# One bank and one ScalarE copy for the transposes of a head pair's first two units

## The reference

```
xn  = layernorm(x)
q, k, v = xn Wq + bq, xn Wk + bk, xn Wv + bv         16 heads of 64
att = softmax(causal(q k^T / 8)) / 8                 512 x 512 per head
y   = (att v, heads side by side) proj
ffn = xn W^T + gate-weighted low-rank experts of ranks 1, 2, 4, 8 (top 1 of 4)
out = x + y + ffn
```

## Time and profile before

| what | value |
|---|---|
| median of three executions | 1382.9 us |
| profiled execution, its own time | 1383.64 us |
| span of its trace | 1381.9 us |
| PE busy | 1364.5 us (99% of the span) |
| PE weight loads busy | 1163.6 us (84%) |
| DVE busy | 1110.2 us (80%) |
| ACT busy | 1076.5 us (78%) |
| POOL busy | 973.1 us (70%) |

### The profile page before, as it was taken

How to read it: one execution, slowest core, us unless ns; L and a number is a source line. 1 busy time by engine, 2 the same in 40 slices (tenths; PEclk the granted TensorE clock), 3 DMA queues, 4 the chain that set the end, 5 groups by cost and what they waited for, 6 DMA issues and landing times.

```text
span 1381.9 us, 34974 instructions
## 1 busy us (share of the span) xinstructions
PE 1364.5 (99%) x11053; PEld 1163.6 (84%) x11053; DVE 1110.2 (80%) x4009; ACT 1076.5 (78%) x3161; POOL 973.1 (70%) x1421
## 2 busy tenths in 40 slices
PE   6999999999999999999999999999999999999998
PEld 5788888888888888888888888888888888888887
DVE  4978878788787887878788787887878878788784
ACT  4887877877787787787878878777787877878784
POOL 6777766777677777767777677776676776677664
PEclk7999999999999999999999999999999999999999
DMA  5444444445445444444454544454454444534441
GB/s 143 98 112 114 106 116 109 108 113 117 108 100 125 107 100 120 109 117 97 111 124 100 122 109 108 107 120 112 93 123 114 102 112 111 123 93 116 115 101 47
DMA packets 113011, 151.41 MB, mean 110 GB/s; under 512 B 18303, under 2 KB 47294, under 8 KB 112830
## 3 DMA queue, kind: packets, MB, share of 16 engines
q1 hardware_dynamic: 112830, 149.17, 45.7%
HBM read 10.69 MB, written 4.19 MB: 11 GB/s over the span
## 4 chain that ended last, share of the span: by engine, by line
PE 96%; DVE 0%; POOL 0%; issue 0%; ACT 0%; DVEq 0%; POOLq 0%
PE zp L1187 22%; PE ptp L1163 20%; PE scores L1151 13%; PE jobp L1066 12%; PE scores L1154 12%; PE outp L1199 7%; PE jobp L1071 6%; PE jobp L1081 1%; PE outp L1208 1%; PE jobp L1086 1%; PE jobp L1224 0%; PE jobp L1076 0%; PE outp L1213 0%; PE outp L1284 0%; POOL prob L582 0%; DVE prob L884 0%
## 5 line engine op out<-in xcount | busy, mean ns | idle before, releaser
L582 POOL TENSOR_TENSOR prob<-prob,rden 128x128 f32<-128x128 f32 (+3 forms) x1024 | 711.7, 722 | 345.9 <-DVE rden L873 344.2
L884 DVE CUSTOM_DVE_ANT_0 prob<-scores,mask 128x128 f32<-128x128 f32 (+3 forms) x1024 | 465.3, 487 | 216.4 <-issue 190.4
L667 ACT ACTIVATE prob<-prob,nmax 128x128 f32<-128x128 f32 (+3 forms) x1024 | 564.3, 555 | 35.2 <-DVE nmax L884 35.1
L1163 PE MATMUL ptp<-ident,prob 128*128 128x128 f32 x2560 | 369.9, 274 | 2.0 <-POOL prob L582 1.1
L1151 PE MATMUL scores<-k_twice,q_parts 128*128 128x128 f32 (+3 forms) x1024 | 331.5, 334 | 2.8 <-DMA k_twice<-k_hi 1.7
L1154 PE MATMUL scores<-k_low,q_parts 128*128 128x128 f32 (+3 forms) x1024 | 322.4, 324 | 0.0
L1163 PEld LDWEIGHTS ptp<-ident,prob 128*128 128x128 f32 x2560 | 294.7, 141 | 30.6 <-issue 7.0
L1187 PE MATMUL zp<-pt,v_sb 128*64 128x64 f32 (+3 forms) x4096 | 307.8, 303 | 0.2 <-ACT pt L678 0.2
L678 ACT ACTIVATE pt<-ptp 128x128 f32<-128x128 f32 (+3 forms) x512 | 220.4, 431 | 111.9 <-PE ptp L1163 111.9
L1187 PEld LDWEIGHTS zp<-pt,v_sb 128*64 128x64 f32 x4096 | 221.5, 137 | 51.5 <-issue 19.3
L1151 PEld LDWEIGHTS scores<-k_twice,q_parts 128*128 128x128 f32 x1024 | 193.2, 189 | 69.0 <-issue 43.8
(11 more groups left out here) (163 smaller groups left out, 1697.2 us busy)
## 6 DMA issues: line engine op xcount, KB each, us to landing
k_twice<-k_hi SPq DMA_DIRECT2D x512, 128.0 KB, 2.3
q_parts<-q_hi SPq DMA_DIRECT2D x256, 128.0 KB, 2.3
q_parts<-q_lo SPq DMA_DIRECT2D x256, 128.0 KB, 2.4
xin<-in_L_attn_x_dram SPq DMA_DIRECT2D x16, 256.0 KB, 3.8
xres<-in_L_attn_x_dram SPq DMA_DIRECT2D x16, 256.0 KB, 3.1
out_dram<-osb SPq DMA_DIRECT2D x15, 256.0 KB, 2.6
pt<-in_L_attn_Wq_dram SPq DMA_DIRECT2D x1, 512.0 KB, 4.5
pt<-in_L_attn_Wk_dram SPq DMA_DIRECT2D x1, 512.0 KB, 4.8
```

The lines of the kernel that those rows point to most:

```text
L582: nc.gpsimd.tensor_tensor(part, part, scale, ALU.mult).then_inc(pn_ready, 1)
L667: nc.scalar.activation(part, part, ACT.Exp, bias=nmax[:, s % NROT, h:h + 1], scale=-1.0, accum_out=den[:, s % NROT, h:h + 1]).then_inc(p_r ...
L884: nc.vector.tensor_tensor_reduce(out=prob[:, s % NROT, h, 0:cols], in0=scores[h][:, 0:cols], in1=mask[:, S - cols:S], scale=-INV_SCALE, sc ...
L1163: done = nc.tensor.transpose(ptp[h][:, P * j:P * j + P], prob[:, s % NROT, h, P * j:P * j + P], ident[:])
```

## The change

For the first two units of a pair (`SHARED = 2`) the transposes of both heads go into `ptp[0]`, side by side: 2 x 128 columns for the first unit, 2 x 256 for the second, which fills the bank. ACT waits for both heads and copies both in one instruction, 256 or 512 columns wide; DVE copies nothing for these units. The third and fourth unit stay as they were. PE's transposes of head 1 wait for nothing of their own in the first two units, since head 0's wait covers the bank; in the third and fourth unit they wait for `pt_ready[1]`, which now counts two copies a pair (`wide`). At a pair's first unit ACT waits for the older pair's head 1 `values` in place of head 0's.

```diff
+SHARED = 2
+    def wide(self, p, n):
+        return self.at(UNITS // 2, 2 * p + n)
             def evacuate_pt(c, s):                                  # ScalarE
-                act.wait_ge(t_ready, c.head(s, 0))
                 i, p = s % NBLK, s // NBLK
                 if i == 0:
-                    wait(act, pv_ready, c.values(p - 2, 0))
+                    wait(act, pv_ready, c.values(p - 2, 1))
+                if i < SHARED:
+                    act.wait_ge(t_ready, c.head(s, 1))
+                    src = ptp[0][:, 0:2 * width(s)].rearrange("p (h j q) -> p h j q", h=2, q=P)
+                    nc.scalar.activation(pt[:, p % 2, :, 0:i + 1, P * i:P * i + P], src, ACT.Copy)\
+                        .then_inc(pt_ready[0], 1)
+                    return
+                act.wait_ge(t_ready, c.head(s, 0))
             def evacuate_pt(c, s):                                  # VectorE
+                i, p = s % NBLK, s // NBLK
+                if i < SHARED:
+                    return
                 dve.wait_ge(t_ready, c.head(s, 1))
-                i, p = s % NBLK, s // NBLK
-                if i == 0:
-                    wait(dve, pv_ready, c.values(p - 2, 1))
...
-            evacuate_pt(c, -3)                                      # VectorE, at the very end
             def transpose(c, s):                                    # TensorE
+                i, p = s % NBLK, s // NBLK
                 for h in range(2):
                     pe.wait_ge(pn_ready, c.head(s, h))
-                    wait(pe, pt_ready[h], c.unit(s - 1))
-                    for j in range(s % NBLK + 1):
-                        done = nc.tensor.transpose(ptp[h][:, P * j:P * j + P], prob[:, s % NROT, h, P * j:P * j + P],
+                    if h == 0:
+                        wait(pe, pt_ready[0], c.unit(s - 1))
+                    elif i >= SHARED:
+                        wait(pe, pt_ready[1], c.wide(p, i - SHARED))
+                    dst = ptp[0][:, h * width(s):(h + 1) * width(s)] if i < SHARED else ptp[h][:, 0:width(s)]
+                    for j in range(i + 1):
+                        done = nc.tensor.transpose(dst[:, P * j:P * j + P], prob[:, s % NROT, h, P * j:P * j + P],
                                                    ident[:])
                     done.then_inc(t_ready, 1)
             def values(c, p, h):                                    # TensorE
-                pe.wait_ge(pt_ready[h], c.unit(NBLK * p + NBLK - 1))
+                pe.wait_ge(pt_ready[h], c.unit(NBLK * p + NBLK - 1) if h == 0 else c.wide(p, NBLK - SHARED))
```

## The result

The changed kernel takes 1391.59 us (median of 6 runs, 1390.09 to 1392.52), the kernel before 1382.95 us in the same series. The ratio is 1.0064, with a 95% interval of 1.0054 to 1.0074: slower by 8.6 us, where 9.9 us were forecast. The profiled execution has a span of 1390.8 us, 8.9 us more than before.

A forecast was written before the change was run, and what follows sets the result against it. PE's own work bounds the kernel, with a DVE, ACT, PE chain tight in pairs 1, 3 and 6. Losses of 0.23, 0.16 and 0.23 us, 0.62 us a batch, add 9.9 us to 1382.9: 1392.8 us, range 1384 to 1400 us.

The forecast's parts named there:

- ACT's copy of the second unit: 512 columns for 256, 0.23 us longer; third unit's load late in pairs 1, 3, 6: 0.62 us a batch, 9.9 us.
- the lower bound: At the stalls, PE's loads lose up to 0.05 us less each: about 0.47 us a batch, +7.5 us.
- the pattern comes back in each batch: Third unit tight in pairs 1, 3 and 6 of every batch, read from pair 1 six batches later.
- ACT's copy of the first unit and the wait for both heads: In pairs 0, 2, 4, 7: 0.14 us lateness plus 0.23 us width, 0.37 of 0.51 us slack; no loss counted.
- The load of pair 0 waits too: Sign at the third unit's first load in pair 0: if it waits, the prediction is wrong.
- DVE's relief: DVE loses two copies a pair, some 0.68 us, which ends in its idle time; counted as nothing.
- The rival in which it reaches the fourth unit's maximum: DVE's saved time starts ACT's exponentials earlier in pairs 1, 3, 6: 1377 us, chance 0.09.
- One sign that I had named for it: ACT's idle time before the fourth unit's exponentials in pair 1 shorter than 0.60 us would show DVE's saving arriving.
- PE's waits of head 1: First two units' waits go, 0.24 us in pair 6; PE then waits at the third unit's transposes: nothing counted.
- The dearer copy: Rival: the second unit's two-head copy costs more than its columns, 0.37 us extra: 1400 us, chance 0.13.
- PE taking it up: Rival: at the third unit's loads PE's queue hides the delay, nothing measurable: 1383 to 1385 us, chance 0.16.
- What the prediction took the rule alone to mean: Giving up bank rotation for half the units would make the third unit wait in every pair; rows said three in eight.

The follow-up runs named there:

- e2: Changed kernel with only the second unit sharing the bank (512 columns in one copy), the first unit copied by head as before: 1391.09 us, ratio 1.0063 to the kernel before.
- e3: Changed kernel, ACT waiting for both heads of the second unit but copying only head 0's 256 columns: 1381.33 us, ratio 0.9993 to the kernel before.
- g2: Changed kernel with the second unit's ACT copy cut to 384 columns: 1387.0 us, ratio 1.0027 to the kernel before.
- g1: Changed kernel with both heads of the second unit put into the second bank, ACT's copy as wide: 1380.84 us, ratio 0.9987 to the kernel before.
- e1: Changed kernel with only the first unit sharing the bank (`SHARED = 1`), the second copied by head as before: 1381.08 us, ratio 0.9987 to the kernel before.
- e4: Kernel before without DVE's head 1 copies of a pair's first two units, ACT and banks as before: 1381.3 us, ratio 0.9990.
- f2: Changed kernel with ACT's wide copy of the second unit put before q_hi instead of behind it: 1418.37 us, ratio 1.026 to the kernel before.

## Why the prediction was right

*ACT's copy of the second unit.* This is the step that carries the result, and it held in place and cause, and nearly in number: three pairs in eight, a load 0.11 us behind the wide copy, the others free in the steady batches. e2, e3, g2 and g1 each show a part of it: the unit, the width, its size, the bank. Of the sizes, 0.23 us in pairs 1 and 6 was 0.186 us, or 0.21 us with the next transpose, which is also 0.03 us late. The copy is 0.01 us shorter than the row I took (587 for 597 ns), and the lead of load over matmul gives 0.03 us, where the forecast gave it nothing and the lower bound up to 0.05 us. Pair 3 was forecast at 0.16 us and lost as much as the others: there the wait for head 1 in the second unit went (0.04 us), PE came earlier, and used up the slack that I had counted. With what that wait gave (0.067 us over two transposes) pair 3 is 0.145 us later in all, near the 0.16 us. That the pattern comes back in each batch was wrong for the first one, which the prediction had not read: its pairs 0, 2 and 4 lose 1.05 us together, of which the sum had nothing. The last batch grows by 0.9 us less than a steady one, and that the two ends nearly cancel is luck.

*ACT's copy of the first unit and the wait for both heads, pairs 0, 2, 4 and 7.* Forecast: 0.37 us of 0.51 us of slack used. Measured: the distance from copy to load in pair 0 fell from 0.63 to 0.23 us, so 0.40 us, of which the first copy's 387 ns in place of 367 are 0.02 us. In the steady batches these pairs' third units lose nothing, but for the 0.09 us in the fourth, and e3 and e1 show that the wait for both heads and the wider first copy cost nothing. The load of pair 0 waits too, a sign that the prediction had named against itself, only in the first batch, where that load stood at the least distance already before the change.

*DVE's relief.* Forecast at nothing; e4 measured a gain of 1.65 us between medians, and 0.045 us a batch in the trace. The rival in which it reaches the fourth unit's maximum fell with e4. One sign that I had named for it was badly chosen: ACT's idle time before those exponentials did shrink in the changed kernel, for ACT's own reasons.

*PE's waits of head 1.* I said that what pair 6 gains comes back in the third unit, on the chain through ACT. It comes back earlier: 0.074 us go, and 0.101 us return at head 1's scores in the next step, which wait for DVE's maximum of the fourth unit. The sum is near nothing, as forecast.

*The dearer copy, and PE taking it up.* Both fell. The 512-column copy over two heads costs 587 ns, no more than the one-head form; and only 0.03 us of each stall was taken up.

The rule of the Trainium skill, Perfetto Trace Analysis, section Optimizing Tensor Performance (Matmuls), to rotate groups through PSUM banks, is borne out here: g1 differs from the changed kernel in the second unit's bank and the waits that guard it, and is 10.8 us faster between medians. What the prediction took the rule alone to mean, a wait of the third unit in every pair, did not come: in the steady batches pairs 0, 2, 4 and 7 share the bank and lose nothing but 0.09 us once.

## What to carry to other kernels

Where one engine is busy all the time, look for the smallest distance between a release and the instruction that it releases, place by place over one period of the program: where it equals the least distance seen anywhere, that work is on the path or at its edge, however idle the releasing engine is on average. Read the first period by itself; here it had three tight places that the others have not. A merged PSUM copy frees its bank later than two small ones; put the group that follows into the other bank. And a swap that takes one instruction off the path can put its neighbour on it: here the copy first cost 27 us more than the stall it removed.

## What was not expected of the hardware

A matmul can start as little as 0.03 us after its weight load (719.60 to 719.63 us in g2), where it starts 0.11 us after it when nothing is late (707.96 to 708.07 us). So a late load delays its matmul by less than it is late itself: the copy of g2 is 0.11 us longer than that of e3, its load as much later, and its matmul 0.08 us. The 512-column ScalarE copy took 587 ns in the changed kernel with a source and a destination over two heads and 599 ns with one head's (L690). That is not the pattern's price: in f2, where the two-head copy stands ahead of q_hi, it takes 599 ns as well. At 256 columns it is 387 ns (two heads, first unit) against 367 ns (one head, second unit of the kernel before); whether that is the pattern or the place in the program is not shown.
